# Local attention with masked maxima on VectorE: the sums of squares ahead of the second scoring, in another bank

## What is computed

```python
qkv = shift_token(x) @ wqkv                # 8 heads of 64, for q, k and v
q = l2norm(q) * qs                         # q / max(norm(q), 1e-12) over the 64 of a head
k = l2norm(k) * ksc
q, k = rotary_xpos(q, k)                   # a rotation and a scale that depend on the token
# windows of 128 tokens; each sees its own window and the one before it
sim = einsum('bhwid,bhwjd->bhwij', bq * 8, bk)
attn = softmax(where(mask, -max, sim))
x = x + (attn @ v) @ wo
```

## Time and profile before

| | us |
|---|---|
| median of 3 runs | 4212.72 |
| lowest, highest | 4208.02, 4218.27 |
| profiled execution, whole time | 4210.37 |
| its span | 4208.6 |
| PE busy in it | 3459.1 |
| DVE busy | 2573.2 |
| ACT busy | 1619.9 |
| POOL busy | 670.4 |

### The profile page before, as it was taken

How to read it: one execution, slowest core, us unless ns; L and a number is a source line. 1 busy time by engine, 2 the same in 40 slices (tenths; PEclk the granted TensorE clock), 3 DMA queues, 4 the chain that set the end, 5 groups by cost and what they waited for, 6 DMA issues and landing times. The chain is left out here.

```text
span 4208.6 us, 76983 instructions
## 1 busy us (share of the span) xinstructions
PE 3459.1 (82%) x32364; PEld 2096.5 (50%) x32428; DVE 2573.2 (61%) x4368; ACT 1619.9 (38%) x1937; POOL 670.4 (16%) x464
## 2 busy tenths in 40 slices
PE   5818899999988999999955589997698789997695
PEld 3403333333333333333433477776587577775575
DVE  4317788777647888776557466664454566663554
ACT  1103556676735566767600233322121233231222
POOL 4400000000000000000000333331122333331131
PEclk9958999999979999999977799998799899998898
DMA  5491000100030000000011100000000000000003
GB/s 167 138 160 28 17 9 16 47 21 9 24 74 24 16 9 9 9 9 16 19 67 60 49 17 17 17 17 1 26 0 19 28 17 15 16 17 1 26 0 120
DMA packets 84257, 142.01 MB, mean 34 GB/s; under 512 B 11025, under 2 KB 42129, under 8 KB 82977
## 3 DMA queue, kind: packets, MB, share of 16 engines
q1 hardware_dynamic: 83952, 137.59, 11.7%
HBM read 94.49 MB, written 42.53 MB: 33 GB/s over the span
## 5 line engine op out<-in xcount | busy, mean ns | idle before, releaser
L529 DVE TENSOR_REDUCE mp<-ps_s 128x2 f32<-128x1024 f32 (+3 forms) x1152 | 1287.7, 1135 | 492.4 <-PE ps_s L585 370.6
L510 ACT ACTIVATE probs<-ps_s 128x1024 f32<-128x1024 f32 (+3 forms) x1152 | 1087.6, 954 | 778.0 <-PE ps_s L613 389.5
L632 PE MATMUL ps_o<-probs,vst 128*32 128x256 f32 (+3 forms) x9216 | 703.0, 377 | 2.3 <-ACT o_sb L500 2.2
L613 PE MATMUL ps_s<-qst,kst 64*128 64x512 f32 (+3 forms) x2304 | 519.1, 447 | 118.1 <-DMA qst<-mrow 50.7
L585 PE MATMUL ps_s<-kst,qst 64*128 64x512 f32 (+3 forms) x2304 | 542.6, 482 | 77.9 <-DMA qst<-null_rows 66.4
L585 PEld LDWEIGHTS ps_s<-kst,qst 64*128 64x128 f32 x2304 | 218.9, 189 | 487.4 <-issue 385.0
L613 PEld LDWEIGHTS ps_s<-qst,kst 64*128 64x128 f32 x2304 | 218.9, 186 | 310.2 <-DVE mp L529 171.8
L632 PEld LDWEIGHTS ps_o<-probs,vst 128*32 128x32 f32 x9216 | 182.5, 108 | 276.6 <-issue 238.5
L488 POOL TENSOR_TENSOR msplit<-negm,mzero 128x16 fp32r<-128x16 f32 x32 | 7.1, 222 | 1849.4 <-DVE negm L536 1849.4
L1210 DVE SCALAR_TENSOR_TENSOR a_t<-a_BP,a_sc,a_tab 128x256 f32<-128x256 f32 x384 | 166.8, 476 | 192.4 <-ACT a_sq L910 192.1
L889 ACT ACTIVATE a_PT<-a_SU 128x1024 f32<-128x1024 f32 (+1 forms) x128 | 122.4, 1009 | 370.2 <-PE a_SU L1006 370.2
(11 more groups left out here) (161 smaller groups left out, 5473.1 us busy)
## 6 DMA issues: line engine op xcount, KB each, us to landing
a_tab<-in_rope SPq DMA_DIRECT2D x32, 512.0 KB, 3.7
q_parts<-pparts SPq DMA_DIRECT2D x32, 256.0 KB
k_parts<-pparts SPq DMA_DIRECT2D x32, 256.0 KB
v_aug<-pvsb SPq DMA_DIRECT2D x32, 256.0 KB, 4.3
kst<-k_parts SPq DMA_DIRECT2D x64, 128.0 KB, 6.5
vst<-v_aug SPq DMA_DIRECT2D x32, 256.0 KB, 10.4
qst<-q_parts SPq DMA_DIRECT2D x64, 128.0 KB, 2.7
o_raw<-o_sb SPq DMA_DIRECT2D x32, 256.0 KB, 2.1
```

What stands on the lines that cost most here:

```text
L510: act.activation(probs[:, s % PR, 2 * hp:2 * hp + 2, off:C], slots[place["score", n] % SR][:, :, off:C], ACT.Exp, scale=float(D) ** -0.5). ...
L529: dve.tensor_reduce(mp[b % 2][:, h:h + 2, cc:cc + 1], slots[place["max", n] % SR][:, :, 0:width], AX.X, ALU.max).then_inc(max_read, 1)
L613: last = pe.matmul(slots[at % SR][:, x, off:C], kst[g % 2][rows, hp, i * P:(i + 1) * P], qst[q_slot(b)][rows, hp, off:C], start=True, stop ...
L632: last = pe.matmul(ps_o[32 * h:32 * h + VW, lo:hi], vst[g % 2][:, i, h * VW:(h + 1) * VW], probs[:, s % PR, h, lo:hi], start=(i == 0 and h ...
```

## The change

Three edits in the local attention layer. On PE, the sums of squares are issued ahead of `score_turned(2k-4)` in place of behind it, and go to bank B7 in place of B6; their wait for `vc_done` becomes one for `nm_done` (from k = 2). The turning of the sums (into B6) comes directly behind `score_turned(2k-4)`, ahead of `turn_max(2k-2)`, and takes over the wait for `vc_done`. On ACT, the copy `sse` reads B7 and comes ahead of `weights(2k-4)`.

```diff
@@ ACT @@
-                if win(2 * k - 4):
-                    weights(2 * k - 4)
                 if live(k):
                     act.wait_ge(ss_done, k + 1)
                     if k >= 1:
                         act.wait_ge(sst_done, k)
-                    act.activation(sse[:, :], B6[:, 0:N2], ACT.Copy).then_inc(sse_done, 1)
+                    act.activation(sse[:, :], B7[:, 0:N2], ACT.Copy).then_inc(sse_done, 1)
+                if win(2 * k - 4):
+                    weights(2 * k - 4)
                 if win(2 * k - 2):
                     turn_max(2 * k - 2)
@@ PE @@
                     values(2 * k + 1)
+                if live(k):
+                    pe.wait_ge(sq_done, 4 * k + 4)
+                    if k >= 2:
+                        pe.wait_ge(nm_done, 2 * k - 2)
+                    for d in range(2):
+                        for g in range(4):
+                            last = pe.matmul(B7[32 * g:32 * g + 32, 0:N2], blocks[:, :], sq[:, g, d, :], start=(d == 0),
+                                             stop=(d == 1), tile_position=(0, 32 * g), skip_group_check=True)
+                    last.then_inc(ss_done, 1)
                 if win(2 * k - 4):
                     score_turned(2 * k - 4)
                 if live(k):
-                    pe.wait_ge(sq_done, 4 * k + 4)
+                    pe.wait_ge(sse_done, k + 1)
                     pe.wait_ge(vc_done, 2 * k + 2)
-                    for d in range(2):
-                        for g in range(4):
-                            last = pe.matmul(B6[32 * g:32 * g + 32, 0:N2], blocks[:, :], sq[:, g, d, :], start=(d == 0),
-                                             stop=(d == 1), tile_position=(0, 32 * g), skip_group_check=True)
-                    last.then_inc(ss_done, 1)
-                if win(2 * k - 2):
-                    turn_max(2 * k - 2)
-                if live(k):
-                    pe.wait_ge(sse_done, k + 1)
                     for a in range(2):
                         last = pe.transpose(B6[:, a * P:(a + 1) * P], sse[:, a * P:(a + 1) * P], id_sb[:, :])
                     last.then_inc(sst_done, 1)
+                if win(2 * k - 2):
+                    turn_max(2 * k - 2)
                 if live(k - 3):
                     weigh(k - 3, 0)
                     weigh(k - 3, 1)
```

## The result

The changed kernel takes 4230.72 us in the median (4225.43 to 4238.90), the kernel before 4214.67 beside it: a ratio of 1.0041, with a 95% interval of 1.0025 to 1.0057. That is +17 us (11 to 24 by the interval), slower. The forecast was 4225, +12.8 us.

What follows compares the result with a forecast made beforehand. One loop of PE, ACT's tail, the weighing, DVE's reciprocals and ACT's copies was taken to bound the kernel. Two layers x (8.6 - 2.2) = +12.8 us on the 4212.7 median gave 4225 us, range 4214 to 4263.

Steps and rivals of the forecast that it cites:

- A: Steady iterations k = 3 to 15: +0.66 us each, clock drops behind the second gap as before; 4225 us, chance 0.45.
- The sums on the loop: PE ahead of the second scoring: no wait hides the sums of squares, +1.01 us per iteration, bounds 0.2 to 1.1.
- ACT's tail: ACT behind the scores: a_sse leaves the tail before the weighing, 0.35 us gained per iteration, bounds 0.27 to 0.40.
- The rest of the steady part: Behind the scores: transposes cost nothing under ACT's 2.3 us; clamp and POOL's power start 1.4 us earlier, winning nothing.
- The first three iterations: k = 0 to 2, no weighing: 0.8 us gained at k = 0, nothing at k = 1, 1.4 at k = 2; 2.2 a layer.
- Rival B: Wider gap before the weighing, 1.63 us, brings a second clock drop each iteration: 36 us on top, 4261; chance 0.27.
- D: Longer iterations meet the clock drop less often, 8 times in 13 instead of 11: 6 us less, 4219; chance 0.23.
- my price of 1.0 us for such a drop: Clock drop behind the 2.11 us gap before L1110: 10 us for ten drops over twelve iterations, 1.0 us each.
- C: In front of L968: late maxima on DVE make a wait that hides the sums; -13.5 us, 4199; chance 0.05.

Runs made afterwards that it cites:

- The cut in the new place: Changed kernel with the eight products of the sums of squares cut to one, ahead of the second scoring: 4200.75 us, ratio 0.9983 to the kernel before.
- the cut in the old place: Kernel before with the eight products of the sums of squares cut to one, behind the second scoring: 4203.92 us, ratio 0.9993 to the kernel before.
- the run with them alone: Kernel before with the changed order on PE and ACT in iterations 0 to 2 only: 4199.57 us, ratio 0.9978 to the kernel before.
- The kernel with the second gap filled: Changed order in k = 0 to 2, maxima copied between exponentials after, plus eight filler products before the factors' turning: 4157.21 us, ratio 0.9881 to the kernel before.

## Why the prediction came out as it did

The mechanism of A, the sums on PE's loop with nothing to hide them, is what happened. That its number is close is luck in part, for what was too small and what was left out nearly cancel.

**The sums on the loop: right in kind, too small.** Forecast 1.01 us, measured 1.10. The row in front of L968 has 0.16 us of idle time, where the row of before shows none; that the step between two kinds of products costs that time was not tested. The cut in the new place confirmed that PE's time there is on the loop, the cut in the old place that it had been hidden.

**ACT's tail: right in kind, too large.** Forecast gain 0.35 us, measured 0.28, just above my lower bound of 0.27. The tail is 2.44 us, not 2.37. The sum of the two terms is 0.82 in place of 0.66, times 26 that is 21.3 us in place of 17.2.

**The rest of the steady part: right.** From the weighing to a_rnx nothing moved, and POOL's power came earlier for nobody.

**The first three iterations: too small.** Forecast 2.2 us a layer, by the run with them alone 9 us in both layers together, 4.5 in each. The changed kernel has the same gain: from a_rnx of k = 0 to that of k = 2 it is 3.1 and 2.2 us shorter than before, 3.2 and 2.0 in the run with them alone. What I left out was the clock, where PE's gaps in front of L1110 are 4.36 to 6.45 us, two to three times the 2.11 us that the prediction took for the longest: at k = 1, where I had nothing, 1.2 and 0.6 us were gained, and iteration 3 gained by the clock behind a_rnx of k = 2.

**The clock.** Rival B, a drop over the weighing, happened in 4 of 26 iterations, not in all and not in none; at 1.7 us each that is 6.8 us. The gap had been forecast at 1.63 us and is 1.85, because L1151 and L1020 run closer together than I had set them (0.74 taken, 0.6 measured) and because of the longer tail. D happened too, with 17 drops behind the second gap in place of 22. But my price of 1.0 us for such a drop was too low. The kernel with the second gap filled has no drop in these iterations, 406.2 us for twelve. Set against the same iterations of that kernel, those without a drop were 0.67 us longer before the change (34.61 and 34.78 against 33.93 and 34.12) and are 1.49 us longer after it (35.18 against 33.69 for the first); the difference is the 0.82 again. So the ten drops of a layer cost 426.7 - 406.2 - 12 x 0.67 = 12.4 us before, 1.2 each. In the changed kernel all drops in the 24 iterations cost 872.7 - 812.4 - 24 x 1.49 = 24.5 us: 3.4 for two over the weighing, 1.4 us each for the fifteen behind the gap. Fewer drops, each dearer, and the new ones: over these 24 iterations the clock costs 25 us before and after, and the 19.3 us are the loop.

**The sum again**, by these parts: 21.3 for the loop, -9 for the first iterations, +6.8 for the drops over the weighing, -3.7 for those behind the gap (24.8 us before, 21.1 after), makes 15 us; the runs say 17, with 11 to 24 in the interval. The forecast of +12.8 was thus too low by 4 us in the loop and by some 3 in the drops, and too high by 5 in the first iterations.

**C** is excluded by the rows: in iterations 0 to 15 no idle time in front of L1142 or L968 is ended by the maxima.

The Trainium skill's sentence that transposes don't count as busy for the gate ("TensorE: Matmul & The Clock Gate", "Part 4: PE-mode transpose") was read one-sidedly in the prediction, which set the new gap with its transposes, 2.4 us, against 2.11 without any. By that sentence the second gap has transposes on both sides, L1097 and L1110 in the first timeline above: 0.66 + 2.10 + 1.09 = 3.9 us, against 0.66 + 1.85 = 2.5 for the gap in front of the weighing. Counted so, the gap that brings a drop in 17 of 26 iterations is still much the longer one, and the other, with a drop in 4 of 26 (and in none with the same gap in the kernel with the cut sums), lies between it and the 0.97 us gap of before, 1.8 us with its transposes, that never did; so the sentence didn't make B the forecast. Idle time alone, 2.10 against 1.85 us, gives the same order, so the gaps don't tell whether transposes count.

The profiled execution of the changed kernel is 20.3 us longer in its span than that of before. The first a_rnx of layer one already lies 4.0 us later (2370.42 against 2366.45), ahead of all but one of the changed iterations, and over the other kernels it lies between 2361 and 2378. Between a_rnx of k = 0 and that of k = 15 the two layers lost 8.5 and 7.7 us, 16.2 together, and that is what the trace gives to the change, less up to 1.6 us for the wait at k = 0, which ends ahead of the first a_rnx.

## What to carry to other kernels

Before moving work off a queue to shorten a tail, ask what hides it where it stands: 1.1 us of PE time under two exponentials cost nothing, and a place where PE doesn't wait made it cost all of its length. A wait is bought back by looking at what the waiter really needs: here the weighing needed one small copy, queued behind two long exponentials that it didn't need, and putting the copy between them gave 35 us, about half of it by the loop and half beside fewer drops of the clock. A change that helps in the first iterations and hurts in the steady ones should be tried for each part alone.

## What the runs showed of the hardware

Behind the idle gap of TensorE in front of the factors' turning, 2.1 us long (2.5 to 2.7 at the first and last of the 13 iterations of a layer), the granted clock fell from 2.4 to 1.2 GHz in 22 of 26 iterations of the kernel before, in 17 of the changed one, in 20 of the one whose steady iterations are those of before, and in 11 and 10 of the two whose weighing starts without a gap. A gap of 1.85 us in front of the weighing did so in 4 of 26 iterations of one kernel, in 9 of 26 of another and in none of a third. Gaps of 0.76, 0.97 and 1.50 us between the scoring and the weighing never did, nor did the second gap filled down to 1.11 us. The length of a gap alone therefore doesn't settle the clock: the same gap brought a drop in one iteration and none in the next. A small change elsewhere in the iteration went with up to a dozen drops more or fewer, of 0.9 to 1.7 us each; what decides it was not separated here.
